# Graph attention layer on one core: g and p from d by one exp each, a third PSUM bank for h, one filler product, new instruction orders up to the end of the first group, and closing sums with the high-value products first

## What is computed

```python
h = maximum(layernorm(x), 0)                 # x: 4096 x 256, fp32
h = h @ W.T                                  # W: 256 x 256
src = h @ a1;  dst = h @ a2
e = leaky_relu(src[:, None] + dst[None, :], 0.2)
e = where(adj == 0, -9e15, e)                # adj: 4096 x 4096, int32
out = x + softmax(e, axis=1) @ h
```

## Time and profile before

| | us |
|---|---|
| median of 3 runs | 384.48 (384.36 to 384.53) |
| profiled execution | 384.67 |
| its span | 382.9 |
| PE busy | 376.8 (98%) |
| DVE busy | 363.9 (95%) |
| ACT busy | 195.1 (51%) |
| POOL busy | 42.0 (11%) |

### The profile page before, as it was taken

How to read it: one execution, slowest core, us unless ns; L and a number is a source line. 1 busy time by engine, 2 the same in 40 slices (tenths; PEclk the granted TensorE clock), 3 DMA queues, 4 the chain that set the end, 5 groups by cost and what they waited for, 6 DMA issues and landing times.

```text
span 382.9 us, 9216 instructions
## 1 busy us (share of the span) xinstructions
PE 376.8 (98%) x3358; PEld 330.7 (86%) x3358; DVE 363.9 (95%) x458; ACT 195.1 (51%) x271; POOL 42.0 (11%) x66
## 2 busy tenths in 40 slices
PE   8999899999999999999999999999999999999996
PEld 6788688888888888888888888888888888888885
DVE  4999999999999999999999999999987999999965
ACT  5899754744443644344445544444446443444330
POOL 3897020000000001110000002100000012100000
PEclk9999999999999999999999999999999999999999
DMA  7922476847676666776676667766665577766503
GB/s 241 370 78 56 130 235 218 287 154 238 217 236 208 205 220 214 243 229 218 220 223 207 209 217 233 236 222 225 215 205 184 168 222 240 232 220 221 165 2 110
DMA packets 27024, 78.22 MB, mean 204 GB/s; under 512 B 3956, under 2 KB 9336, under 8 KB 27000
## 3 DMA queue, kind: packets, MB, share of 16 engines
q1 hardware_dynamic: 25712, 74.72, 60.9%
q0 software_dynamic: 1280, 3.16, 2.2%
q10 hardware_dynamic: 8, 0.00, 0.0%
HBM read 73.66 MB, written 4.21 MB: 203 GB/s over the span
## 4 chain that ended last, share of the span: by engine, by line
PE 96%; ACT 1%; DVE 1%; DMA 1%; issue 1%; ACTq 0%
PE ps L1390 87%; PE ps L1214 2%; PE ps L1229 2%; PE ps L1235 2%; PE ps L1240 2%; DMA a_rows<-a 1%; PE ps L1179 1%; PE ps L1195 1%; DVE rows_sb L1119 0%; ACT c_row L494 0%; ACT h_sb L468 0%; ACT L620 0%; ACT p_hi L504 0%; ACTq L479 0%; DVE inv_den L1115 0%
## 5 line engine op out<-in xcount | busy, mean ns | idle before, releaser
L1390 PE MATMUL ps<-v_sb,p_hi 128*128 (+2 forms) x2048 | 251.8, 273 | 1.0 <-ACT p_hi L504 0.9
L514 ACT ACTIVATE p_hi<-p_sb,gp 128x1024 f16<-128x1024 f32 x126 | 144.4, 1149 | 166.6 <-DVE p_sb L785 140.0
L1390 PEld LDWEIGHTS ps<-v_sb,p_hi 128*128 128x128 f16 x2048 | 199.6, 98 | 26.9 <-issue 1.2
L792 DVE SCALAR_TENSOR_TENSOR p_lo<-p_sb,gp,p_hi 128x1024 f16<-128x1024 f32 x126 | 160.8, 1277 | 7.1 <-ACT p_hi L514 6.7
L785 DVE SCALAR_TENSOR_TENSOR p_sb<-c_row,gp,adj_sb 128x1024 f32<-128x1024 uint32 (+1 forms) x126 | 160.5, 1278 | 0.0
L1390 PE MATMUL ps<-v_sb,p_lo 128*128 (+1 forms) x1024 | 142.7, 273 | 0.0
L1390 PEld LDWEIGHTS ps<-v_sb,p_lo 128*128 128x128 f16 x1024 | 100.0, 98 | 12.7 <-DVE p_lo L792 0.2
L452 POOL DMA_DIRECT2D out<-rows_sb x24 | 13.0, 541 | 263.1 <-DVE rows_sb L1086 262.9
L401 POOL TENSOR_SCALAR hn_sb<-x_sb,moments,rstd 128x256 f32<-128x256 f32 x17 | 21.3, 1261 | 4.3 <-DVE rstd L734 3.4
L744 DVE SCALAR_TENSOR_TENSOR hnt_lo<-ps,hnt_hi 128x256 f16<-128x256 f32 x32 | 12.9, 410 | 0.5 <-ACT hnt_hi L484 0.5
L1229 PE MATMUL ps<-w_hi,hnt_hi 128*128 128x258 f16 x64 | 12.5, 277 | 0.5 <-ACT h_sb L468 0.4
(11 more groups left out here) (85 smaller groups left out, 87.3 us busy)
## 6 DMA issues: line engine op xcount, KB each, us to landing
adj_sb<-adj_t SPq DMA_DIRECT2D x128, 512.0 KB, 4.8
x_sb<-x SPq DMA_DIRECT2D x7, 512.0 KB, 8.3
out<-rows_sb POOLq DMA_DIRECT2D x24, 128.0 KB, 4.3
c_row<-c_flat SPq DMA_DIRECT2D x3, 512.0 KB, 6.1
out<-rows_sb SPq DMA_DIRECT2D x8, 128.0 KB, 1.7
x_sb<-x SPq DMA_DIRECT2D x2, 256.0 KB, 3.8
c_row<-s_flat SPq DMA_DIRECT2D x1, 512.0 KB, 3.8
w_nat<-w SPq DMA_DIRECT2D x1, 256.0 KB, 2.8
```

What stands on the lines that cost most here:

```text
L514: nc.scalar.activation(p_hi[:, u % R, :], p_sb[:, u % R, :], ACT.Copy, scale=p_scale[:, bass.ds(t, 1)])\
L792: nc.vector.scalar_tensor_tensor(out=p_lo[:, u % R, :], in0=p_sb[:, u % R, :], scalar=p_scale[:, bass.ds(t, 1)], in1=p_hi[:, u % R, :], op ...
L1390: return nc.tensor.matmul(ps[:, k, 0:width], part[:, u % R, k * P:(k + 1) * P], v_sb[:, bass.ds(t, 1), v, 0:width], start=start, stop=stop ...
```

## The change

- BUSY fillers ahead of the first transposes: one instead of three. ACT computes w_hi's first half, the columns of a, the second half, then the standard deviations of tiles 2 and 3, and only then normalises tile 0; tile 1 is normalised by POOL.
- h goes to three banks (6, 7, 4); d's bound uses banks 5 and 2 instead of 4 and 5.
- Who normalises which tile, and who copies which pair of v, is new: ACT 15 tiles, POOL 16, DVE 1; v's high part by POOL for all pairs but 18, 20 and 24.
- All orders up to the end of group 0 are new. POOL computes exp_scale and den_scale late, between copies of v.
- g and p: no `gp_args`. ACT takes exp straight from h_sb's d column with scale and bias, once for g and once for p (`exp_g`, `exp_p`); DVE computes p's bias (`p_bias`). The splits of tiles 30 and 31 stand behind the bound of d on DVE.
- c_col and its transposition come later in group 0.
- The closing sums issue for each row block first the products with v's high part (6), which complete the denominator, and later those with the low part (3); DVE takes denominators from PSUM in between. Row block 4 is scaled by ACT, x is added by POOL, and ACT's queue stores it. The least denominator is sought before the last rows, its comparison is on POOL.

```diff
-    ROWS_TOGETHER = ((0, 2), (2, 4), (4, 6), (6, 7), (7, 8))
+    FIRST_OF_LAST = (NG - 1) * RB
+    SIDE_ROW = 4
...
-        bank_w, bank_n, bank_d, bank_e = 4, 1, 4, 5
-        bank_h = 6
+        bank_w, bank_n, bank_d, bank_e = 4, 1, 5, 2
+        banks_h = (6, 7, 4)
+        HB = len(banks_h)
...
-                if t >= 2:
-                    pe.wait_ge(*kept(t - 2))
+                if t >= HB:
+                    pe.wait_ge(*kept(t - HB))
...
-            def exp_gp(tiles, n):
-                act.wait_ge(gp_args_ready, n)
-                nc.scalar.activation(gp[:, :, tiles], gp_args[:, :, tiles], ACT.Exp).then_inc(gp_ready, 1)
+            def exp_g(t0, t1):
+                act.wait_ge(c_bias_ready, 1)
+                act.wait_ge(h_kept, t1)
+                nc.scalar.activation(g_col[:, t0:t1], h_sb[:, t0:t1, F + 1], ACT.Exp,
+                                     bias=exp_bias[:, 0:1], scale=exp_scale[:, 1:2]).then_inc(g_ready, 1)
...
-            nc.vector.tensor_scalar(gp_args[:, 0, 0:R], h_sb[:, 0:R, F + 1], exp_scale[:, 1:2],
-                                    exp_bias[:, 0:1], ALU.mult, ALU.add).then_inc(g_args_ready, 1)
-            dve.wait_ge(g_args_ready, 1)
-            nc.vector.tensor_scalar(gp_args[:, 1, 0:R], gp_args[:, 0, 0:R], 0.25, math.log(P_UP), ALU.mult, ALU.add)\
-                .then_inc(gp_args_ready, 1)
-            value_lo(10)
+            nc.vector.tensor_scalar(p_bias[:], exp_bias[:], 0.25, math.log(P_UP), ALU.mult, ALU.add).then_inc(p_bias_ready, 1)
+            split_hn_lo(30)
+            split_hn_lo(31)
...
+            act.wait_ge(rows_free, FIRST_OF_LAST + RB)
+            act.wait_ge(last_inverse_ready, SIDE_ROW + 1)
+            act.wait_ge(rows_done, FIRST_OF_LAST + SIDE_ROW + 1)
+            late = FIRST_OF_LAST + SIDE_ROW
+            nc.scalar.activation(rows_sb[:, SIDE_ROW, 0:F], ps[:, SIDE_ROW, 0:F], ACT.Copy, scale=inv_den[:, late:late + 1])\
+                .then_inc(row_scaled, 1)
+            act.wait_ge(side_row_ready, 1)
+            act.dma_start(out_v[:, late, :], rows_sb[:, SIDE_ROW, 0:F]).then_inc(last_stored, 16)
...
+            pool.wait_ge(row_scaled, 1)
+            nc.gpsimd.tensor_tensor(rows_sb[:, SIDE_ROW, 0:F], rows_sb[:, SIDE_ROW, 0:F], x_sb[:, FIRST_OF_LAST + SIDE_ROW, :],
+                                    ALU.add).then_inc(side_row_ready, 1)
+            pool.wait_ge(den_least_ready, 1)
+            pool.wait_ge(den_taken, RB)
+            nc.gpsimd.tensor_scalar(den_is_low[:], den[:, T - 1:T], den_least[:, 0:1], den_low[:, 0:1], ALU.min, ALU.is_lt)\
+                .then_inc(low_ready, 1)
...
-            keep_busy(bank_h, 3)
+            keep_busy(banks_h[0], 1)
...
+            def closing_sums(t, n, closing):
+
+                def high_values(k):
+                    for u in range(U - closing, U):
+                        if k == 0:
+                            pe.wait_ge(p_lo_ready, n + (u + 1))
+                        product(u, t + u, k, p_hi, 0, False, False)
+                        done = product(u, t + u, k, p_lo, 0, False, False)
+                    done.then_inc(den_summed, 1)
+
+                def low_values(k):
+                    pe.wait_ge(den_taken, k + 1)
+                    for u in range(U - closing, U):
+                        done = product(u, t + u, k, p_hi, 1, False, u == U - 1)
+                    done.then_inc(rows_done, 1)
+
+                high_values(0)
+                high_values(1)
+                high_values(2)
+                high_values(3)
+                low_values(0)
+                low_values(1)
+                high_values(4)
+                high_values(5)
+                low_values(2)
+                low_values(3)
+                high_values(6)
+                low_values(4)
+                high_values(7)
+                low_values(5)
+                low_values(6)
+                low_values(7)
```

753 lines of the change are left out of this document (397 added, 356 removed).

## The result

| | before | changed |
|---|---|---|
| median, beside each other | 384.43 (384.06 to 384.53, 8 runs) | 386.91 (384.87 to 388.04, 8 runs) |
| ratio | | 1.0059, 95% interval 1.0047 to 1.0071 |
| profiled execution | 384.67 | 386.62 |
| its span | 382.9 | 384.9 |

The change makes the kernel 0.6% slower, about 2.5 us. The forecast was 383.2, and its range ended at 384.5. The changed kernel's runs also scatter over 3 us where those of before lie within 0.5.

The account below looks back on a forecast made before the run. TensorE's product rate was taken as the bound, so only time ahead of tile 3 and behind the last product could change. 0.6 + 0.25 + 0.4 = 1.25 us off 384.67 gave 383.4, as median 383.2; range 382.4 to 384.5.

Parts of the forecast that it names:

- Filler: Ahead of the first transposes: two of three fillers go, tile 0 starts later, a loss of 0.15 us.
- the third rival: At the start, idle TensorE sets the clock's rise back 4.2 us, costing 2.1: 385.3; chance 0.12.
- 6 us of activity: At TensorE's start: the clock rises after some 6 us hardly idle; begun anew at 8.4, it ends at 14.5 to 14.8.
- Projection order and third bank: Before the spread of d: 0.75 of 1.22 us of waits go; with the filler's -0.15 the stage gains 0.6.
- moves behind the last transposed tile: ScalarE before the spread of d: one copy of h moves back, part of about 0.6 us less work there.
- g and p by one exp each: Between the spread of d and tile 3: gains 0.25 us, ends 0 and 0.4.
- small exp more: ScalarE ahead of the first product: one extra exp, so weights 0.2 earlier bring the product only about 0.1 earlier.
- c_col later: In group 0: transposition three tiles or 8 us later, costed at nothing; without cover up to 2 us once.
- The closing sums: Behind the last product: earlier denominators, last row's store and flag gain 0.4 us, ends 0.1 and 0.6.
- The second rival: Ahead of the spread of d: the projections win nothing, or c comes late; 383.8 to 384.4, chance 0.3.

Follow-up runs that it names:

- a_fill3: The changed kernel with three fillers ahead of the first transposes instead of one; 385.19, ratio to before 1.0023.
- b_fill1_again: b_fill1 unchanged, profiled a second time; 384.7 in one run.
- a_copies: a_fill3 with GpSimd's copies of v for tiles 10 and 12 moved ahead of its normalisation of tile 25; 384.36, ratio 0.9995.
- b_fill1: The kernel before with one filler instead of three; 385.8, ratio 1.0038.
- b_gp: The kernel before with g and p by one exp each, in the order of before; 384.93, ratio 1.0011.
- a_late: a_copies with GpSimd's last two copies of v (tiles 28 and 30) behind its stores of c; 384.77, ratio 1.0009.
- a_act: a_copies with ScalarE's exp of p behind the second exp of c, and the copies for tiles 28 and 30 on ScalarE; 383.84, ratio 0.9989.
- b_tail: The kernel before with the new closing part alone; 383.98, ratio 0.9987.
- a_first_gp: a_act with g and p of tiles 0 to 3 by one exp of arguments that VectorE writes; 383.42, ratio 0.9972.

## Why the prediction was wrong

- **Filler**, forecast -0.15 "with the clock rising at 10.5 as before": this is the step that failed most. It measured -1.7 (changed kernel against a_fill3). I had put the whole mechanism into the third rival, with the right formula (half of the delay) and a chance of 0.12; the profiled step came 2.56 late, just at the point from which that rival decides, and the median of 386.91 is above even its 385.3, which still counted on the other terms. The 6 us of activity by which it was priced are not borne out: with three fillers the step lay anywhere from before 5.2 to 10.5. The argument against it was that the kernel before also had a pause at the transposes and still rose. But there it stood for some 0.3 us between transposes and products, with three fillers straight ahead of them; in the changed kernel it stood for 0.96 behind one. The Trainium skill (TensorE: Matmul & The Clock Gate, Part 1) says that an idle engine falls back to the throttled default; the granted 0.50 behind the 1.12 of idle in b_fill1_again agrees, the full rate behind 1.27 of idle in a_copies shows that such a pause is not always enough. That page also says that the step's place varies from run to run, which the 13.1 and 12.2 of one kernel show and which the forecast's single 10.5 left out. What in a pause decides is open: b_fill1 had 0.78 of idle behind its one filler and was at full rate behind it.
- **Projection order and third bank**, forecast +0.6: the size was nearly there, and hidden. With three fillers the spread came at 35.66, 0.44 ahead of before (0.24 ahead of b_fill1, whose clock stepped at the same place); with two GpSimd copies out of VectorE's way at 34.55 to 35.19. The step that failed is the price of a copy of v on GpSimd: I took its 0.66 there, and had no term for the subtractions beside it, 0.27 more each on VectorE. And the copy of h that "moves behind the last transposed tile" was counted as a gain alone, although the bound on d reads h: `d_most` went from 0.56 ahead of the spread to 0.52 behind it, and the exp of c came 0.26 later behind the spread. No experiment moved that copy, so whether it held `d_most` isn't shown: `d_most` starts at 37.87, where both ScalarE's copies of h (37.81) and VectorE's splits ahead of it (37.95) end.
- **g and p by one exp each**, forecast +0.25 with ends 0 and 0.4: it measured -0.48 in b_gp by the medians and -0.17 in its trace, beyond the lower end by either. The half of the term that was to come from VectorE's dropped instructions ahead of tile 2 was right (0.29 of the 0.35). The other half had the wrong sign: the first product was to come 0.1 earlier and came 0.46 later in b_gp, 0.20 of it in the changed kernel's order. I counted VectorE's two instructions as saved and one "small exp more" on ScalarE as 0.1. The exps took 0.38 each against 0.20 for one of eight elements, and stood in front of the exp of c and the first high part. The Trainium skill (ScalarE: Activation LUTs, What ACT_TABLE_LOAD costs) puts an instruction with immediate scale and bias at 186 ns and 0.83 ns per element, and each operand that points to a column at 93 more. By it, as an estimate, the exp of gp_args costs 0.19 and each new one 0.38; the rows agree with both.
- **Low part of tile 0's weights**: no term. GpSimd's last two copies wait for the copies of h, which come just then, and cost 0.7 there (4.24 to 3.53 in a_late and a_act; in a_act tile 3 comes 0.70 sooner behind the first product).
- **c_col later**, forecast 0: TensorE has no gap behind tile 3, so it was right.
- **The closing sums**, forecast +0.4: 0.42 in b_tail, and 0.4 in the two spans. Right, and for the reasons given. The add on GpSimd was bounded at 1.37 and took 0.72.
- **The second rival** had "a new wait arises in the written-out order, since four engines are nearly full there", and then limited it to a gain of nothing. A full stretch can also lose.

In sum, in the two profiled executions: 1.69 for the filler (the spread, against a_fill3), less the 0.44 that the projections won in spite of the stretched subtractions; 0.26 from the spread to the exp of c, 0.20 from there to the first product, 0.77 in tile 0 (0.70 of it by the two copies), less 0.27 in tiles 1 and 2; 0.2 in the sums; less 0.4 at the end: 2.0, the difference of the spans. The medians differ by 2.5; no profile shows the other 0.5, and the changed kernel's slowest runs were never the profiled ones.

## What to carry to other kernels

A filler product is not taken out on the strength of one profile: the clock's step moved by 5 us between executions of kernels with the same start, so its removal is tried over several runs, and the medians count. Before a copy is moved to GpSimd, look at what VectorE does at that moment. An instruction that reads two tensors from SBUF, beside two such copies (1.17 alone) grew by 0.7 to 1.25, so the copy's place matters more than its engine's idle time; beside instructions that read fewer, the copies cost nothing here but for one open case (the 0.57 in a_first_gp). And an instruction on four elements is all fixed cost (0.38 for four where 0.20 made eight): what merging two such is worth depends on the order, 0.46 on the way to the first product in one, 0.11 in the other, where nothing of it was left at tile 3. Last, when work is moved behind a landmark, look for who reads its result: `d_most` reads the copies of h, it ended up behind the spread with them, and no term had asked after it.
